# A macaron transformer kernel: the experts' second product as three products of high and low halves

## The reference

```
def _mlp(x, w1, w2, w3):
    h = jax.nn.silu(x @ w1.T) * (x @ w3.T)
    return h @ w2.T
...
combine = (one_hot(indices, E) * weights[..., None]).sum(axis=1)
for e in range(E):                      # E = 8
    y = y + _mlp(xt, w1[e], w2[e], w3[e]) * combine[:, e:e + 1]
z = _mlp(xt, sw1, sw2, sw3)             # the shared expert
return (y + z).reshape(shape)
```

## Time and profile before

| | us |
|---|---|
| median of 3 runs | 1342.8 |
| lowest and highest | 1339.66 and 1343.28 |
| the profiled execution | 1338.12 |
| its span in the trace | 1336.3 |

### The profile page before, as it was taken

The page is one execution under the profiler, slowest core; times in us unless marked ns, Lnnn a source line. Parts: engine busy times, 40 slices in busy tenths (PEclk is TensorE's granted clock), DMA queues, the critical chain, the costliest instruction groups (busy, mean ns, idle before and its releaser), DMA issues.

```text
span 1336.3 us, 16868 instructions
## 1 busy us (share of the span) xinstructions
PE 1213.5 (91%) x5959; PEld 786.4 (59%) x6008; DVE 907.9 (68%) x1754; ACT 641.8 (48%) x1183; POOL 235.5 (18%) x201
## 2 busy tenths in 40 slices
PE   5998878999899889799999979789998996979998
PEld 3676444567666555566667744446776664546665
DVE  6766856455467698987765667665465667989765
ACT  4544444544422497962234325554443227969322
POOL 3001000000020075651000010000000102928210
PEclk9999899999999989899999989999999997979999
DMA  6213121000101121220200032100001101222120
GB/s 227 56 32 93 44 58 34 2 1 1 64 1 64 40 80 31 91 95 0 72 24 0 22 90 62 54 3 1 1 1 64 44 20 60 76 58 79 64 72 9
DMA packets 32580, 63.19 MB, mean 47 GB/s; under 512 B 4176, under 2 KB 19824, under 8 KB 32304
## 3 DMA queue, kind: packets, MB, share of 16 engines
q1 hardware_dynamic: 32496, 62.11, 14.6%
HBM read 54.16 MB, written 8.45 MB: 47 GB/s over the span
## 4 chain that ended last, share of the span: by engine, by line
PE 72%; DVE 12%; ACT 7%; issue 3%; POOL 2%; DMA 2%; SPq 1%; another core or an unknown queue 0%; DVEq 0%; POOLq 0%; ACTq 0%
PE bank L1529 13%; PE bank L1530 13%; PE bank L1531 13%; PE bank L1698 9%; PE bank L1538 6%; PE bank L1848 4%; DVE a_mx L1410 3%; ACT n_part L1077 3%; PE bank L1607 3%; PE bank L1763 2%; PE bank L1668 2%; POOL n_hc L830 2%; ACT n_da L1069 2%; DMA a_k<-stack_dram 2%; PE bank L1734 2%
## 5 line engine op out<-in xcount | busy, mean ns | idle before, releaser
L1254 DVE SCALAR_TENSOR_TENSOR f_hl<-bank,f_hh 128x512 fp32r<-128x512 f32 x192 | 131.8, 689 | 129.7 <-ACT f_hh L904 129.0
L904 ACT ACTIVATE f_hh<-bank 128x512 fp32r<-128x512 f32 x192 | 114.8, 598 | 188.0 <-PE bank L1607 149.8
L966 ACT ACTIVATE m_sl<-bank 128x512 f32<-128x512 f32 x144 | 86.1, 599 | 235.2 <-PE bank L1531 234.8
L830 POOL TENSOR_TENSOR n_hc<-n_h,n_cs 128x512 f32<-128x512 f32 x128 | 159.9, 1278 | 177.8 <-DVE n_h L1500 173.2
L1529 PE MATMUL bank<-xT_h,mw_h 128*128 128x512 f32 x288 | 161.1, 559 | 3.5 <-DVEq L532 2.7
L1500 DVE TENSOR_TENSOR_SCAN n_h<-n_da,bank 128x512 f32<-128x512 f32 x128 | 149.7, 1206 | 9.1 <-PE bank L1538 6.3
L1698 PE MATMUL bank<-m_h,mw 128*128 128x512 f32 x288 | 145.6, 594 | 0.0
L1321 DVE TENSOR_TENSOR m_t<-m_sl,bank 128x512 f32<-128x512 f32 x128 | 87.9, 687 | 78.7 <-PE bank L1531 77.5
L1410 DVE TENSOR_REDUCE a_mx<-bank 128x1 f32<-128x384 f32 (+3 forms) x176 | 106.0, 637 | 43.2 <-PE bank L1804 40.8
L1848 PE MATMUL bank<-n_hc,ident 128*128 128x512 f32 x256 | 135.0, 614 | 0.2
L983 ACT ACTIVATE a_p<-bank 128x1024 f32<-128x1024 f32 (+3 forms) x128 | 88.0, 704 | 89.5 <-PE bank L1739 48.4
(11 more groups left out here) (243 smaller groups left out, 2305.1 us busy)
## 6 DMA issues: line engine op xcount, KB each, us to landing
n_cs<-c_dram SPq DMA_DIRECT2D x32, 512.0 KB, 3.6
m_c<-comb_dram SPq DMA_DIRECT2D x28, 512.0 KB, 5.1
a_q<-stack_dram SPq DMA_DIRECT2D x8, 512.0 KB, 4.3
a_k<-stack_dram SPq DMA_DIRECT2D x16, 256.0 KB, 5.1
stage_fw<-in_fw_dram SPq DMA_DIRECT2D x6, 512.0 KB, 8.7
stack_dram<-R SPq DMA_DIRECT2D x16, 192.0 KB, 2.8
w_stage<-in_mw_dram SPq DMA_DIRECT2D x9, 256.0 KB, 2.6
stack_dram<-R SPq DMA_DIRECT2D x16, 128.0 KB, 2.6
```

The costliest lines, as they stand in the source:

```text
L830: n_hcs.by(nc.gpsimd.tensor_tensor(n_hc[:, i % 4, :], n_h[:, i % 4, :], n_cs[:, j % C_RING, i // 2 % 2, :], ALU.mult))
L1254: f_lo.by(V.scalar_tensor_tensor(f_h[1][:, i % 4, :], bank[:, i % 3, :], 0.0, f_h[0][:, i % 4, :].bitcast(F32), ALU.max, ALU.subtract))
```

## The change

The second product is made by `product` too, of halves: its moving operand is `m_hh` (the high half, by ACT with a Copy to fp32r) and `m_hl` (`m_h` minus `m_hh`, by POOL). Its weights are split anew in each unit, one MLP every two steps, into a ring of three (`m_w2`): ACT writes the high half (128x256), POOL the rest. The second product now follows three steps behind the projections (`W2_LAG`), not two. `m_t` is gone: DVE's first multiplication writes over the projection in PSUM, so PE may write the projections of step i only when the second multiplication of step i - 2 is done (`m_hs`), where it waited for the first (`m_ts`). `m_h` has two buffers, not three, and DVE writes it only when POOL has made the low half of step i - 2. The combine rows have one home for both p, and a transfer for p = 1 waits until the unit before has read the rows in it.

```diff
+W2_RING, W2_LAG = 3, 3
...
+            def weight_rest(k, j):
+
+                n = MLPS * k + j
+                pool.wait_ge(m_wh.sem, m_wh.at(k, j))
+                if n >= W2_RING:
+                    pool.wait_ge(m_s2.sem, m_s2.at(k, 2 * (j - W2_RING) + 1))
+                m_wl.by(nc.gpsimd.tensor_tensor(m_w2[:, n % W2_RING, 1], flat(mw2[:, MLP_ORDER[j]]),
+                                                m_w2[:, n % W2_RING, 0].bitcast(F32), ALU.subtract))
...
                     for i in range(MSTEPS):
+
+                        if i % 2 == 0:
+                            weight_rest(k, i // 2)
+                        pool.wait_ge(m_hi.sem, m_hi.at(k, i))
+                        if i >= 3 or p == 1:
+
+                            pool.wait_ge(m_s2.sem, m_s2.at(k, i - 3))
+                        m_lo.by(nc.gpsimd.tensor_tensor(m_hl[:, i % 3, :], m_h[:, i % 2, :],
+                                                        m_hh[:, i % 3, :].bitcast(F32), ALU.subtract))
                         hand_over(u, i - MOE_LAG * p)
...
                         m_silu.by(act.activation(m_sl[:, i % 2, :], bank[:, i % 2, :], ACT.Silu))
+                    if i >= 1:
+                        high_half(k, p, i - 1)
+                    if i % 2 == 1:
+                        weight_half(k, i // 2)
                     hand_over(u, i - MOE_LAG * p)
...
+                    up = other_projection(p, m)
                     if e < EXPERTS:
-                        m_ts.by(V.tensor_tensor(m_t[:, m, :], m_sl[:, m, :], other_projection(p, m), ALU.mult))
+                        m_ts.by(V.tensor_tensor(up, m_sl[:, m, :], up, ALU.mult))
...
-                    if i >= 3 or p == 1:
-
-                        dve.wait_ge(m_s2.sem, m_s2.at(k, i - 3))
+                    if i >= 2 or p == 1:
+
+                        dve.wait_ge(m_lo.sem, m_lo.at(k, i - 2))
...
-                for i in range(MSTEPS + 2):
+                for i in range(MSTEPS + W2_LAG):
...
-                        if i >= 4 or (i < 2 and p == 1):
-
-                            pe.wait_ge(m_ts.sem, m_ts.at(k, i - 4))
-                        elif i >= 2:
+                        if i >= 2 or p == 1:
+
                             pe.wait_ge(m_hs.sem, m_hs.at(k, i - 2))
...
-                        m_s2.by(mm(bank[:, 6, :], mw2[:, e, m, :], m_h[:, i2 % 3, :],
-                                   start=i2 == 0, stop=i2 == MSTEPS - 1))
+                        m_s2.by(product(bank[:, 6, :], [m_w2[:, slot, c, m * P:(m + 1) * P] for c in range(2)],
+                                        [m_hh[:, i2 % 3, :], m_hl[:, i2 % 3, :]],
+                                        start=i2 == 0, stop=i2 == MSTEPS - 1))
```

More of the change, by code:

```diff
@@ L279, in program @@
         m_sl = sb("m_sl", [P, 2, T], F32, s)
-        m_t = sb("m_t", [P, 2, T], F32, s)
-        m_h = sb("m_h", [P, 3, T], F32, s)
+        m_h = sb("m_h", [P, 2, T], F32, s)
+        m_w2 = sb("m_w2", [P, W2_RING, 2, 2 * P], F32R, s)
         m_yT = sb("m_yT", [P, T], F32, s)
[L283 to L288, removed]
+        sb("m_rest", [P, 4, T], F32, s)
+        m_cb = sb("m_cb", [P, 2, T], F32, s)
+        m_hh = sb("m_hh", [P, 3, T], F32R, s)
+        m_hl = sb("m_hl", [P, 3, T], F32R, s)
+        sb("n_end", [P, 4, T], F32, s)
+        m_ca = sb("m_ca", [P, EXPERTS - 2, T], F32, s)
+        m_c = [m_ca[:, 2 * n:2 * n + 2, :] for n in range(3)] + [m_cb[:]]
         s.close()
@@ L426, in program @@
         m_s2 = sig("m_s2", "moe", MSTEPS)
+        m_hi = sig("m_hi", "moe", MSTEPS)
+        m_lo = sig("m_lo", "moe", MSTEPS)
+        m_wh = sig("m_wh", "moe", MLPS)
+        m_wl = sig("m_wl", "moe", MLPS)
         m_y = sig("m_y", "moe", 1)
@@ L969, in moe, with high_half, weight_half @@
                 m_y.by(act.activation(m_yT[:], bank[:, 6, :], ACT.Copy))
+            def high_half(k, p, i):
+                act.wait_ge(m_hs.sem, m_hs.at(k, i))
+                if i >= 3 or p == 1:
+                    act.wait_ge(m_s2.sem, m_s2.at(k, i - 3))
+                m_hi.by(act.activation(m_hh[:, i % 3, :], m_h[:, i % 2, :], ACT.Copy))
+            def weight_half(k, j):
+                n = MLPS * k + j
+                if n >= W2_RING:
+                    act.wait_ge(m_s2.sem, m_s2.at(k, 2 * (j - W2_RING) + 1))
+                m_wh.by(act.activation(m_w2[:, n % W2_RING, 0], flat(mw2[:, MLP_ORDER[j]]), ACT.Copy))
             def mha(u, k):
@@ L1690, in moe @@
                         m_b.by(product(other_projection(p, m), [mw[c][:, e, 2 + m, :] for c in range(2)], x))
[L1691 to L1694 removed]
+                    if i >= W2_LAG:
+                        i2 = i - W2_LAG
+                        j, m = divmod(i2, 2)
+                        slot = (MLPS * k + j) % W2_RING
+                        pe.wait_ge(m_wl.sem, m_wl.at(k, j))
+                        pe.wait_ge(m_lo.sem, m_lo.at(k, i2))
                         if i2 == 0 and p == 1:
                             pe.wait_ge(m_y.sem, m_y.at(k - 1, 0))
[L1698 to L1699 removed]
+                        m_s2.by(product(bank[:, 6, :], [m_w2[:, slot, c, m * P:(m + 1) * P] for c in range(2)],
+                                        [m_hh[:, i2 % 3, :], m_hl[:, i2 % 3, :]],
+                                        start=i2 == 0, stop=i2 == MSTEPS - 1))
                     if i == 1:
```

12 lines of the change are left out of this document (5 added, 7 removed).

## The result

The changed kernel takes **1403.7 us** (median of 4 runs, 1400.6 to 1406.5) beside 1343.0 us (1339.7 to 1346.0) for the kernel before on the same chip: a ratio of 1.046, 95% interval 1.044 to 1.048. It is slower by 60.7 us, where 45 were forecast: inside the range, 15.7 above the point. The profiled execution has a span of 1404.7 us; its mean granted clock is 0.947 (before 0.963).

What follows compares the result with a forecast made beforehand. PE was taken to bound expert units. Four p=0 units at +9.6, three p=1 at +2.6 and the last at -0.8 gave +45 us on the profiled 1338.1; with 4.7 for the median, 1388 us, range 1358 to 1411.

Steps and rivals of the forecast that it cites:

- PE's work: In 144 expert-unit steps, PE's second product as three fp32r matmuls takes 0.70 us instead of 0.86: -23 us.
- the walk: Timing expert-unit operations one by one through PE, ACT, DVE and POOL; a steady step is 2.10 us.
- The rest of the weights: POOL's 128x256 subtraction for the weight split, taken at 0.70 us, between 0.64 and 1.28.
- Part 4: In p=0 units POOL's four powers queue behind low halves of steps 8 to 11, delaying PE: +6.35 us each.
- Part 3: End of units without router work: last second product ends 4.95 us after the last projection matmul's issue, +2.35 us.
- Part 6: DVE's Newton operations and ranks wait for POOL: 2.5 and 1.25 us; p=0 units +3.75, three p=1 units +2.5.
- the two bounds: POOL between DVE's tiny operations: every gap, Newton 3.3 us, ranks 1.9; only once, 1.25 and 0.6.
- case (c): Rival: POOL gets in at every gap between DVE's tiny operations; 1396 us, 20%.
- The clock: PE falls to 1.2 GHz after new idle times, 7 falls of 1.8 us, besides case (c): 1409 us, 8%.
- (a): Faster rival: POOL's low half costs 0.69 us instead of 1.28, deciding point about 0.9; 1334 us, 7%.
- (b): Rival: POOL's queue alone costs time, no DVE waits beyond it; +23 us, 1366 us, 25%.
- (d): Rival: a wash, the powers fall into the 0.5 us a step POOL has spare; 1343 us, 5%.

Runs made afterwards that it cites:

- the PSUM runs: Changed kernel with small results kept in PSUM: for Newton and router operations 1384.6 us, for Newton operations alone 1394.6 us.
- the run without them: Changed kernel with powers as multiplications, Newton and router small results in PSUM, and the last MLP's second product in f32: 1342.7 us.
- the last experiments: Changed kernel, small results in PSUM, split only at some places: 44 MLPs 1334.7 us, 56 MLPs 1341.2 us, 32 MLPs 1341.7 us.

## Why the prediction was right, point by point

In the traces a p = 0 unit lost 11.7 us on average (forecast 9.6), a p = 1 unit with a successor 3.8 (2.6), and the last unit gained 0.1 (0.8): 58 us instead of 45 in the units. The signs that it named are there: second products at 0.23 us from start to start, POOL busy without a gap from 394.88 to 410.18 us in unit 6, Newton operations near 1 us.

- **PE's work, -23.** Right. Silus of unit 7's steady steps stand 2.07 us apart (448.64, 450.72, 452.79, 454.86) against the 2.10 of the walk. The last unit, with nothing in its way and its end in f32, is 2.9 us shorter than before (37.5 us, in five of the runs); 16 x 0.16 = 2.6.
- **The rest of the weights, 0.70.** Measured 0.74; the low half 1.30 for 1.28. The steady step keeps up, on an edge as said.
- **Part 4, the powers, 6.35 a unit.** The order and the sizes of PE's waits (1.08, 0.48, 1.16 us) follow the walk. The price measured alone is 18.2 / 4 = 4.6 with 4 x 0.21 us left in. It lies below the 6.35, as it should, since the walk also held the longer end, which stays; the two parts of the 6.35 were not measured apart.
- **Part 3, the end, 2.35 a unit.** Right in kind, too small: Q(17) ends 5.4 us behind M(17) in unit 7, not 4.95, and taking the split off the end gave 22.1 us, not 8 x 1.85 = 15. The step missed the clock, and what runs beside the last two low halves: the Mamba unit's own rows, 3.05 instead of 1.11 us. The last unit was to gain 0.8 and gained 0.1.
- **Part 6, the port, 2.5 and 1.25.** The sum, 4 x 3.75 + 3 x 2.5 = 22.5, came near the 19.1 measured, but that is luck: its parts were off in both directions, and the 19.1 holds clock falls that this part did not count. Newton waits 2.56 us more, as taken, but gives only 1.1 to 1.3 back when freed, as rows then collide. The ranks were taken at the middle and are at the upper bound: 1.19 and 1.52 us instead of 0.42 each, 1.87 more, 2.5 a unit with what follows. Which of the two bounds holds was open; the trace shows the full alternation of case (c). Here the Trainium skill (SBUF — State Buffer, "SBUF: two separate sides") states a lock for the whole instruction; the trace agrees, with Newton's first operation ending at 375.96 and POOL's at 375.95 us. That the two engines then take turns, one instruction each, is what these rows add.
- **The clock.** This was left out of the sum and put at 8% as an addition to case (c), 7 falls of 1.8 us. In the profiled execution it is four falls of 2.0 to 2.7 us at the ends of the p = 0 units, smaller ones at two other ends (granted clock 0.86 and 0.79 over 9 and 8 us), and three near step 5: up to some 17 us by the count above. This is the term of the sum that was put at nothing and was not nothing, and by size it covers the distance of 15.7 us from the forecast. How much of the 15.7 it is stays open, since the end and the rows also cost more than in the walk and no run took the clock away alone.
- **Rivals.** (a) falls on its own condition: the low half costs 1.30, not below 0.9. The run with POOL's operations at 0.21 shows that its mechanism is sound (short operations of POOL leave PE's gain), but at 0.21 us and not at its 0.69, so that 1330 lies near its 1334 proves no more. (b) falls with the PSUM runs, (d) with the powers. (c) with part of its clock falls describes what happened better than the forecast's own case: full alternation, a time between its 1396 and 1409, and falls at more places than it named. The forecast's 1388 took the middle of two bounds. The range's lower end has a slip: 0.06 us less for each weight part does not take (b) from 1366 to 1358.

What stays open: if the three losses were all there are, the run without them would stand PE's 20.5 us (128 steps of 0.16) below the kernel before, at 1322; it is at 1342.7. Rows under the subtractions (10 us, by the last experiments) is half of this. The rest, some 10 us, was not taken apart; by the unit times about 7 of it lie in the p = 0 units, 2 of these in a clock fall in unit 18.

## What to carry to other kernels

Before you hand an elementwise job to a "free" POOL, place each of its instructions against DVE's: a DVE operation with two inputs in SBUF, and a tensor_scalar from SBUF to SBUF, however small, can stand until POOL's current one ends, and a run of tiny ones pays that price once each. Add what the new idle times do to PE's clock: here they came in the same places as the waits and cost up to some 17 us. An average load that fits (here 1.67 us of a 2.07 us step) says nothing about bursts, the end of a loop, or the work that already has a date on that engine. Such a trade can still pay if it is made place by place: with 44 of 72 MLPs split it gained 0.5%, with all 72 it lost 4.6%.

## What I had not expected of the hardware

- DVE and POOL alternate strictly when both have work ready: Newton operations of 0.16 us lasted 1.18, 0.66 and 1.21 us, each to within 0.02 us of the end of POOL's.
- A DVE tensor_scalar with one tensor input in SBUF (rows, 128x128, four in 1.11 us) stands in the same way: 2.62 to 3.05 us. The multiplications of 128x512 with one PSUM input, beside the same subtractions, keep their 0.69 us, and so do the statistics, which read one SBUF input: in unit 7 four of them take 0.86 us from 430.91 on beside a subtraction that runs to 431.43, and all 96 in the run take 0.27 to 0.30 us each.
- POOL's power of 128x8 costs 1.64 us, the multiplication of the same tiles 0.21.
